# Layer 0 of a four-layer graph network: the order of the messages and the adjacency blocks on TensorE and ScalarE

## The chip, the core and the metric

One core of a Trainium2 chip runs the whole program in one launch. The metric is the device time of that launch in microseconds (us), as the median of repeated runs. The engines are PE (TensorE, matmuls), DVE (VectorE), ACT (ScalarE), POOL (GpSimd) and SP (SyncE, which here only starts transfers). Each has its own instruction queue and works it off in order; between engines there are only semaphores.

## The reference, cut to what matters

Four graph layers follow each other on 6250 nodes with 128 features and 106250 edges, sorted by target node. Each adds its result to x and normalizes the rows:

```python
edge_index = jnp.stack([src, dst])
x = _layernorm(x + _L0_gnn_ref(x, src, dst, edge_weight, L0_gnn_kernel, L0_gnn_bias), axis=-1)
x = _layernorm(x + _L1_gnn_ref(x, L1_gnn_bases, L1_gnn_relation_base_weights, src, dst, edge_type_64), axis=-1)
x = _layernorm(x + _L2_gnn_ref(x, edge_index, edge_type_2, ...), axis=-1)
x = _layernorm(x + _L3_gnn_ref(x, edge_index, L3_gnn_W1, L3_gnn_b1, L3_gnn_W2, L3_gnn_b2), axis=-1)
```

The change lies in layer 0, which sums over the *source* nodes what it reads at the targets:

```python
def _L0_gnn_ref(inp, edge_row, edge_col, edge_val, kernel, bias):
    support = jnp.matmul(inp, kernel)
    messages = edge_val[:, None] * support[edge_col]
    output = jax.ops.segment_sum(messages, edge_row, num_segments=N_NODES)
    return output + bias
```

The last layer is a graph convolution with two passes over the same edges, `segment_sum(h[src] * norm)`. The kernel computes both passes as dense products with an adjacency matrix, and that matrix is built during layer 0.

## The kernel before

**The loop of layer 0.** The edges lie in 832 tiles of 128. `Fori(0, NBODY)` runs over 52 bodies of 16 tiles; a body has four steps (`FSTEPS`), a step four tiles (`FT`) and two groups of two tiles (`FHALF`). All engines run this loop side by side, each with its own list.

What a step k of body i does for the messages:

- DVE makes `hits`, `sel` and `wS` (lines 1550 to 1560, `sel_ready`): which window column and which source row an edge has, with its weight. Then it finds duplicates of a source within a tile (1563, 1569) and writes the row numbers for the scatter (1573), which waits for `scatter_through`.
- PE, `window_by_edge` (1070): eight fp32 matmuls (four as written; the profile counts each fp32 matmul twice) give C, the weights of the window's nodes in each edge row, into bank 0 or 1. ACT, `keep_window` (723), copies C to SBUF.
- SP loads the window's rows of the support table (498). PE, `rows_to_add` (1080), multiplies C by them: the rows to add, bank 4 or 5, semaphore `messages`.
- ACT, `keep_rows` (728), copies them to SBUF. It waits for `scatter_through`: POOL must have come to the last scatter of step k-1, so that the scatters of step k-2, which used the same half of the buffer, have landed.
- POOL (629) issues four scatters with addition, one into each of four tables in HBM. Scatter t waits until the scatter of the same table of the step before has landed.

What it does for the adjacency, for each of its two groups n:

- DVE (1582, 1583, `ohot_ready`) makes one-hot masks in bf16, two tiles per group. There are two sets of mask buffers, so the masks of a group wait until the matmuls of the group two before are through (`ab_built`).
- PE, `build_adjacency` (1091), multiplies them in six matmuls into banks 3, 6 and 7. Each bank waits until ACT has copied the group before out of it (`ab_kept`).
- ACT, `keep_adjacency` (741), copies the three banks into a kept half in bf16, six copies per step.
- At the end of the body ACT starts the store of the half, 2352 KB (758). The two halves take turns; `adj_stored` guards their reuse.

Once a body DVE makes the type mask (1588) after the masks of step 0, PE multiplies it by the relation weights (`body_weights`, 1100) in step 1, and DVE reduces the result at the end of the body (1592). SP loads edge types (487, after the type mask of the body before) and source rows (491, after `sel_ready` of the body before), 512 KB each.

**Order around the change.** Each engine's order is written by hand. PE: `window_by_edge(0)`, and then for each step `build_adjacency(k)`, `window_by_edge(k + 1)`, in step 1 `body_weights`, `rows_to_add(k)`. ACT: `keep_window(0)`, and then for each step `keep_adjacency(k)`, `keep_window(k + 1)`, `keep_rows(k)`. DVE: selection and index write of step k, then its two groups of masks.

Of the kernel before, what the change touches and what calls it, by code (L numbers as in the profile page):

```python
# [49 lines left out]
FSTEPS = BODY // FT  # L50
# [57 lines left out]
def gnn_program(nc, src, src_row, dst, type2, type64, weight, x, xT0, k0, bias0, bases, rel_weights,  # L108
# [4 lines left out]
    with ctx:  # L113
# [3 lines left out]
        def sem(name):  # L117
            return ctx.enter_context(nc.semaphore(name))
# [214 lines left out]
        adj_stored = [sem(f"adj_stored{k}") for k in range(2)]  # L333
# [366 lines left out]
        def _(act):  # L700
# [19 lines left out]
            def keep_window(i, k):  # L720
                act.wait_ge(c_summed, i * FSTEPS + (k + 3))
                act.wait_ge(messages, i * FSTEPS + (k + 3))
                nc.scalar.activation(C[k % 2], bank[k % 2][0:W, :], ACT.Copy).then_inc(c_kept, 1)

            def keep_rows(i, k):
                act.wait_ge(messages, i * FSTEPS + (k + 5))
                act.wait_ge(scatter_through, i * FSTEPS + (k + 3))
                nc.scalar.activation(msg[k % 2].rearrange("p t f -> p (t f)"), bank[4 + k % 2][:, :],
                                     ACT.Copy).then_inc(msg_kept, 1)
# [6 lines left out]
            def keep_adjacency(i, u, k):  # L736
                for n in range(FHALF):
                    at = k * FHALF + n
                    for j, (bk, ha, hb) in enumerate(H_BANKS):
                        act.wait_ge(ab_built, i * (NHB * RING) + (NHB * (at + 2) + j + 1))  # L740
                        nc.scalar.activation(half_kept[u][:, ha:hb, at * W:(at + 1) * W],  # L741
                                             bank[bk][:, 0:(hb - ha) * W].rearrange("p (h w) -> p h w", w=W),
                                             ACT.Copy).then_inc(ab_kept, 1)
# [3 lines left out]
            with act.Fori(0, NCHUNK) as c:  # L747
                for u in range(2):
                    i = c * 2 + u
                    keep_window(i, 0)  # L750
                    act.wait_ge(adj_stored[u], c * 16 + 16)
                    for k in range(FSTEPS):
                        keep_adjacency(i, u, k)
                        if k < FSTEPS - 1:
                            keep_window(i, k + 1)
                        keep_rows(i, k)
                    act.wait_ge(ab_kept, i * (NHB * RING) + NHB * (RING + 1))
                    act.dma_start(adj[bass.ds(c * P, P), u * HB * HALF_COLS:(u + 1) * HB * HALF_COLS],
                                  half_kept[u].rearrange("p h c -> p (h c)")).then_inc(adj_stored[u], 16)
# [114 lines left out]
        def _(pe):  # L874
# [190 lines left out]
            def window_by_edge(i, k):  # L1065
                g = i * FSTEPS + k
                pe.wait_ge(sel_ready, g + (FSTEPS + 1))
                pe.wait_ge(c_kept, g + 1)
                for t in range(FT):
                    last = nc.tensor.matmul(bank[k % 2][0:W, t * P:(t + 1) * P], wS[:, k % 2, t, :], sel[k % 2][:, t, :],  # L1070
                                            start=True, stop=True)
                last.then_inc(c_summed, 1)

            def rows_to_add(i, k):
                g = i * FSTEPS + k
                pe.wait_ge(c_kept, g + 3)
                pe.wait_ge(xwin_in[k], i * (16 * FHALF) + 16 * FHALF)
                pe.wait_ge(msg_kept, g + 1)
                for t in range(FT):
                    last = nc.tensor.matmul(bank[4 + k % 2][:, t * P:(t + 1) * P], C[k % 2][:, t * P:(t + 1) * P],  # L1080
                                            xwin[k][t // GT], start=True, stop=True)
                last.then_inc(messages, 1)

            def build_adjacency(i, k):
                for n in range(FHALF):
                    at = k * FHALF + n
                    pe.wait_ge(ohot_ready, i * RING + (at + 1))
                    for j, (bk, ha, hb) in enumerate(H_BANKS):
                        pe.wait_ge(ab_kept, i * (NHB * RING) + (NHB * at + j + 1))
                        for t in range(GT):  # L1090
                            last = nc.tensor.matmul(bank[bk][:, 0:(hb - ha) * W], lo_hot[n * GT + t],  # L1091
                                                    hw_hot[n * GT + t][:, ha * W:hb * W], start=t == 0, stop=t == GT - 1)
                        last.then_inc(ab_built, 1)

            def body_weights(i):

                pe.wait_ge(hot_ready, i + 2)
                pe.wait_ge(alpha_ready, i + 1)
                for t in range(BODY):
                    last = nc.tensor.matmul(bank[2][:, t * NB * NPART:(t + 1) * NB * NPART], type_hot[:, t * P:(t + 1) * P],  # L1100
                                            relw_parts[:, :, :].rearrange("r b n -> r (b n)"), start=True, stop=True)
                last.then_inc(alpha_summed, 1)

            pe.wait_ge(relw_ready, 1)
            with pe.Fori(0, NBODY) as i:
                window_by_edge(i, 0)
                for k in range(FSTEPS):
                    build_adjacency(i, k)
                    if k < FSTEPS - 1:
                        window_by_edge(i, k + 1)  # L1110
                    if k == 1:
                        body_weights(i)
                    rows_to_add(i, k)
            pe.wait_ge(ab_kept, NHB * (NG + 1))
            flag = pe.value_load(flag_i[0:1, 0:1], min_val=0, max_val=1)
            with pe.If(flag != 0):
# [575 lines left out]
```

## Time and profile before

| | |
|---|---|
| median of 3 runs | 5966.51 us (5962.67 to 5968.96) |
| profiled execution | 5968.96 us, span 5967.3 us |
| mean granted clock of PE in the span | 0.717 |
| busy in the span: PE, DVE, ACT, POOL | 3830.2, 2201.3, 1009.9, 3073.7 us |
| loop of layer 0 | about 148 to 1922 us of the span |
| in it busy: PE, DVE, ACT, POOL | 1230.1, 1049.1, 745.7, 1309.9 us |
| in it DMA share, bytes moved | 0.63, 142 GB/s |

The span reaches from the first to the last instruction. Busy times are sums over instructions. The granted clock is a share of 2.4 GHz: 1.0 means 2.4 GHz, 0.5 means 1.2 GHz. A row of a timeline gives the start, the duration, engine and line, the operation, what it writes and reads, how many instructions are merged in it, and in brackets the idle time of the engine before it with what ended it. An engine name with a q (ACTq, SPq) is a queue that starts transfers. Lines are those of the kernel before.

### The profile page before, as it was taken

The numbers are of one execution on the slowest core, as the hardware profiler recorded it, in microseconds if no ns is written. First come the engines' busy times: TensorE is split into PE (matmuls) and PEld (weight loads), VectorE is DVE, ScalarE is ACT, GpSimd is POOL, SyncE is SP. The second block draws the span as 40 slices with busy tenths as digits, with TensorE's granted clock in tenths as the row PEclk, the third lists the DMA queues.
The fourth block names the chain that finished last, engine by engine and source line by source line (L and its number), as shares of the span: only waits on it lengthen the run. The fifth ranks groups of instructions, "written<-read, shape, count | busy, mean of one in ns | idle before, by whom it ended". The sixth has DMA issues, their size and how long they took to land. (4 is left out here: it accounts for less than half of the span.)

```text
span 5967.3 us, 90251 instructions
## 1 busy us (share of the span) xinstructions
PE 3830.2 (64%) x20675; PEld 2557.1 (43%) x20676; DVE 2201.3 (37%) x8525; ACT 1009.9 (17%) x2045; POOL 3073.7 (52%) x2549
## 2 busy tenths in 40 slices
PE   4677676676766244444454344444444999989998
PEld 3344333344333233433343333434334566656664
DVE  5566555565555433334343112222222111111122
ACT  2444443444443100000000000000000000000000
POOL 3777777777777666666666566666665000000000
PEclk7777767767676567677667555555555999989999
DMA  7666666666666511111111111111111666666664
GB/s 242 140 143 139 142 153 144 138 143 139 139 152 131 139 44 52 46 51 46 50 47 47 41 42 46 44 46 43 46 44 49 209 205 206 207 198 204 205 206 141
DMA packets 382424, 693.89 MB, mean 116 GB/s; under 512 B 56824, under 2 KB 233889, under 8 KB 371568
## 3 DMA queue, kind: packets, MB, share of 16 engines
q1 hardware_dynamic: 190180, 373.66, 20.9%
q0 software_dynamic: 176272, 185.39, 17.8%
q10 hardware_dynamic: 15804, 133.26, 5.5%
q14 instruction: 143, 1.17, 0.1%
q8 instruction: 25, 0.41, 0.0%
HBM read 474.67 MB, written 220.82 MB: 117 GB/s over the span
## 5 line engine op out<-in xcount | busy, mean ns | idle before, releaser
L589 POOL DMA_INDIRECT rows<-t,idx_ring x1664 | 1642.2, 987 | 953.5 <-issue 468.9
L629 POOL DMA_INDIRECT sums<-rows,idx_ring x832 | 1368.8, 1645 | 501.2 <-DMA sums<-rows,idx_ring 258.8
L927 PE MATMUL bank<-S,rows 128*128 128x192 f32 (+1 forms) x3328 | 914.6, 418 | 730.7 <-DVE arena L1264 485.6
L927 PEld LDWEIGHTS bank<-S,rows 128*128 128x128 f32 x3328 | 767.6, 291 | 862.2 <-DVE arena L1264 514.3
L1091 PE MATMUL bank<-arena 128*128 128x384 bf16 (+1 forms) x2496 | 675.0, 424 | 567.5 <-ACT acc L741 283.2
L1025 PE MATMUL bank<-alpha,arena 128*128 128x384 bf16 x5460 | 902.3, 327 | 0.0
L1025 PEld LDWEIGHTS bank<-alpha,arena 128*128 128x128 bf16 x5460 | 535.6, 98 | 353.9 <-issue 5.6
L1091 PEld LDWEIGHTS bank<-arena 128*128 128x128 bf16 x2496 | 242.1, 115 | 921.1 <-ACT acc L741 354.8
L924 PE MATMUL bank<-S,ones 128*1 128x24 f32 x1664 | 132.4, 210 | 714.8 <-DVE acc L1264 603.9
L1583 DVE TENSOR_SCALAR arena<-S 128x1176 bf16<-128x1176 int16 x832 | 455.8, 548 | 0.0
L1481 DVE TENSOR_TENSOR acc<-acc,bank 128x24 f32 x832 | 149.7, 180 | 802.8 <-issue 484.1
L1262 DVE TENSOR_TENSOR alpha<-alpha,bank 1x24 f32 x416 | 69.9, 168 | 916.9 <-remote 626.7
L924 PEld LDWEIGHTS bank<-S,ones 128*1 128x1 f32 x1664 | 68.0, 88 | 760.9 <-DVE acc L1264 639.3
L1582 DVE TENSOR_SCALAR arena<-S,arena 128x128 bf16<-128x128 int16 x832 | 238.9, 287 | 375.0 <-PE bank L1091 341.3
L1264 DVE TENSOR_TENSOR arena<-arena,bank 128x192 f32 x416 | 147.6, 355 | 605.4 <-issue 253.2
L666 POOL DMA_DIRECT2D arena<-xp_d x7 | 3.8, 559 | 703.6 <-DMA xp_d<-arena 703.6
L1070 PE MATMUL bank<-shared,wS 128*24 128x128 f32 x1664 | 321.8, 359 | 32.1 <-DVE wS L1558 32.1
L692 POOL DMA_DIRECT2D out<-xcur x12 | 9.1, 754 | 635.3 <-DVE xcur L1406 595.4
L1080 PE MATMUL bank<-rows,arena 24*128 24x128 f32 x1664 | 305.0, 335 | 0.0
L741 ACT ACTIVATE acc<-bank 128x384 bf16<-128x384 f32 (+1 forms) x624 | 277.2, 503 | 36.2 <-PE bank L1091 13.0
L741 ACT ACTIVATE xcur<-bank 128x384 bf16<-128x384 f32 (+1 forms) x624 | 275.4, 502 | 35.2 <-PE bank L1091 12.7
L1080 PEld LDWEIGHTS bank<-rows,arena 24*128 24x128 f32 x1664 | 258.1, 233 | 54.1 <-issue 52.6
(152 smaller groups left out, 3400.3 us busy)
## 6 DMA issues: line engine op xcount, KB each, us to landing
alpha<-adj SPq DMA_DIRECT2D x260, 672.0 KB, 4.3
adj<-xcur ACTq DMA_DIRECT2D x26, 2352.0 KB
adj<-acc ACTq DMA_DIRECT2D x26, 2352.0 KB
arena<-src_row SPq DMA_DIRECT2D x104, 512.0 KB
rows<-adj SPq DMA_DIRECT2D x52, 672.0 KB, 4.4
S<-adj SPq DMA_DIRECT2D x52, 672.0 KB, 4.3
arena<-type SPq DMA_DIRECT2D x52, 512.0 KB
rows<-t,idx_ring POOLq DMA_INDIRECT x1664
```

The lines of the kernel that those rows point to most:

```text
L589: nc.gpsimd.indirect_dma_start(out=rows[:, k, t, :], out_offset=None, in_=tables[p], in_offset=bass.IndirectOffsetOnAxis(ap=idx_ring[:, k, ...
L629: nc.gpsimd.indirect_dma_start(out=sums_t[t], out_offset=bass.IndirectOffsetOnAxis(ap=idx4[:, k, t:t + 1], axis=0), in_=msg[k % 2][:, t, : ...
L741: nc.scalar.activation(half_kept[u][:, ha:hb, at * W:(at + 1) * W], bank[bk][:, 0:(hb - ha) * W].rearrange("p (h w) -> p h w", w=W), ACT.C ...
L924: nc.tensor.matmul(count_at(k), ones[:, 0:1], of_group[:, t, 0:W], start=t == 0, stop=t == GT - 1)
L927: last = nc.tensor.matmul(bank[k % 2][:, 0:width], rows[:, k, t, :], of_group[:, t, 0:width], start=t == 0, stop=t == GT - 1)
L1025: last = nc.tensor.matmul(bank[c][:, 0:CHUNK_COLS].rearrange("p (s c) -> p s c", s=2), x_parts[:, q * PIECE_H + hh, part, :], adj_slot[q][ ...
L1070: last = nc.tensor.matmul(bank[k % 2][0:W, t * P:(t + 1) * P], wS[:, k % 2, t, :], sel[k % 2][:, t, :], start=True, stop=True)
L1080: last = nc.tensor.matmul(bank[4 + k % 2][:, t * P:(t + 1) * P], C[k % 2][:, t * P:(t + 1) * P], xwin[k][t // GT], start=True, stop=True)
L1091: last = nc.tensor.matmul(bank[bk][:, 0:(hb - ha) * W], lo_hot[n * GT + t], hw_hot[n * GT + t][:, ha * W:hb * W], start=t == 0, stop=t == ...
L1481: nc.vector.tensor_tensor(to, to, bank[c][:, n * W:(n + 1) * W], ALU.add).then_inc(added[p], 1)
L1582: nc.vector.tensor_scalar(lo_hot[n * GT + t], iota_hw[:, 0:P], lo_f[:, e], None, ALU.is_equal)
L1583: last = nc.vector.tensor_scalar(hw_hot[n * GT + t], iota_hw, hwi[:, e], None, ALU.is_equal)
```

## The change

On ACT, `keep_adjacency(i, u, k)` goes behind `keep_window(i, k + 1)` and `keep_rows(i, k)`, and the wait for the earlier store goes with it. On PE, `build_adjacency(i, k)` goes behind `window_by_edge(i, k + 1)`, `body_weights(i)` and `rows_to_add(i, k)`. DVE's, SP's and POOL's lists stay as they are, and so do all buffers and semaphores.

```diff
@@ -748,12 +748,13 @@
                 for u in range(2):
                     i = c * 2 + u
                     keep_window(i, 0)
-                    act.wait_ge(adj_stored[u], c * 16 + 16)
                     for k in range(FSTEPS):
-                        keep_adjacency(i, u, k)
                         if k < FSTEPS - 1:
                             keep_window(i, k + 1)
                         keep_rows(i, k)
+                        if k == 0:
+                            act.wait_ge(adj_stored[u], c * 16 + 16)
+                        keep_adjacency(i, u, k)
                     act.wait_ge(ab_kept, i * (NHB * RING) + NHB * (RING + 1))
                     act.dma_start(adj[bass.ds(c * P, P), u * HB * HALF_COLS:(u + 1) * HB * HALF_COLS],
                                   half_kept[u].rearrange("p h c -> p (h c)")).then_inc(adj_stored[u], 16)
@@ -1104,13 +1105,14 @@
             pe.wait_ge(relw_ready, 1)
             with pe.Fori(0, NBODY) as i:
                 window_by_edge(i, 0)
-                for k in range(FSTEPS):
-                    build_adjacency(i, k)
-                    if k < FSTEPS - 1:
-                        window_by_edge(i, k + 1)
+                for k in range(FSTEPS - 1):
+                    window_by_edge(i, k + 1)
                     if k == 1:
                         body_weights(i)
                     rows_to_add(i, k)
+                    build_adjacency(i, k)
+                rows_to_add(i, FSTEPS - 1)
+                build_adjacency(i, FSTEPS - 1)
             pe.wait_ge(ab_kept, NHB * (NG + 1))
             flag = pe.value_load(flag_i[0:1, 0:1], min_val=0, max_val=1)
             with pe.If(flag != 0):
```

## Rows read from the trace of the kernel before

**Rows 1.** Busy times by stretch: PE, PEld, DVE, ACT, POOL, granted clock, DMA share, GB/s.

```profile
148.00:1922.00 1774.00, 1230.10 (x6358) 697.69 (x6358) 1049.12 (x4245) 745.74 (x1591) 1309.90 (x796) 0.71 0.63 142
```

**Rows 2.** Groups by line, 148 to 1922 us: busy us, mean ns, idle before.

```profile
L629 POOL DMA_INDIRECT sums<-rows,idx_ring x796 | 1310.1, 1646 | 465.4 <-DMA sums<-rows,idx_ring 251.4 <-issue 201.5 <-DVE idx_ring L1573 9.1
...
L1588 DVE TENSOR_SCALAR arena<-arena,iota_p 64x2048 bf16<-64x2048 int32 x49 | 66.4, 1355 | 0.0
...
L1592 DVE TENSOR_REDUCE alpha<-bank 128x384 f32 x50 | 27.4, 547 | 0.0
```

**Rows 3.** Waits, 148 to 1922 us: who for whom, us in total, times, longest.

```profile
ACT rows L728 <- POOLq L628: 691.8, 161, 10.1
...
POOL sums L629 <- DMA sums<-rows,idx_ring: 251.4, 144, 5.7
...
POOL sums L629 <- ACT rows L728: 3.4, 11, 0.3
```

**Rows 4.** Timeline of ACT from 1006 us: keep_rows and copies behind it.

```profile
1006.50 0.60 ACT L728 ACTIVATE rows<-bank 128x512 f32<-128x512 f32 x1 [8.86 <-POOLq L628]
...
1009.73 0.49 ACT L741 ACTIVATE xcur<-bank 128x384 bf16<-128x384 f32 x1
```

**Rows 5.** Timeline of PE from 1007 us.

```profile
1007.55 2.14 PE L1091 MATMUL bank<-arena 128*128 128x408 bf16 x6 [8.36 <-ACT xcur L741]
...
1011.14 0.56 PE L1100 MATMUL bank<-relw_parts,arena 64*128 64x24 bf16 x16
...
1015.77 1.05 PE L1070 MATMUL bank<-shared,wS 128*24 128x128 f32 x8
1016.76 1.15 PE L1080 MATMUL bank<-rows,arena 24*128 24x128 f32 x8
1017.84 1.17 PE L1091 MATMUL bank<-arena 128*128 128x408 bf16 x6
...
1024.25 2.07 PE L1080 MATMUL bank<-rows,arena 24*128 24x128 f32 x8
1026.26 1.90 PE L1070 MATMUL bank<-shared,wS 128*24 128x128 f32 x8
```

**Rows 6.** Timeline of DVE from 1009 us.

```profile
1009.95 0.25 DVE L1582 TENSOR_SCALAR arena<-S,arena 128x128 bf16<-128x128 int16 x1 [1.73 <-PE bank L1091]
...
1011.25 0.24 DVE L1550 TENSOR_TENSOR hits<-iota_w,rel 128x96 f32<-128x96 f32 x1
...
1012.01 0.24 DVE L1558 TENSOR_TENSOR wS<-hits,wgt 128x96 f32<-128x96 f32 x1
...
1013.57 0.17 DVE L1573 TENSOR_TENSOR idx_ring<-dup,arena 128x4 int32<-128x4 f32 x1
```

**Rows 7.** Timeline of POOL around a store.

```profile
1029.71 1.55 POOL L629 DMA_INDIRECT sums<-rows,idx_ring  x1 [0.30 <-issue]
...
1043.83 1.74 POOL L629 DMA_INDIRECT sums<-rows,idx_ring  x1 [6.79 <-issue]
```

**Rows 8.** Timelines of SP's queue, ACT's queue and POOL, two bodies.

```profile
420.39 0.52 SPq L487 DMA_DIRECT2D arena<-type  x1
427.15 0.34 ACTq L758 DMA_DIRECT2D adj<-acc  x1
434.90 1.55 POOL L629 DMA_INDIRECT sums<-rows,idx_ring  x1 [1.40 <-DMA sums<-rows,idx_ring]
...
1028.79 0.53 SPq L487 DMA_DIRECT2D arena<-type  x1
1029.43 0.37 ACTq L758 DMA_DIRECT2D adj<-xcur  x1
```

**Rows 9.** Timeline of PE: builds after idle times of 2.2 to 2.9 us.

```profile
379.08 1.99 PE L1091 MATMUL bank<-arena 128*128 128x408 bf16 x6 [2.85 <-ACT xcur L741]
...
450.17 1.59 PE L1091 MATMUL bank<-arena 128*128 128x408 bf16 x6 [2.23 <-ACT xcur L741]
...
684.85 1.26 PE L1091 MATMUL bank<-arena 128*128 128x408 bf16 x6 [2.40 <-issue]
```

## The prediction

> **What bounds the kernel now.** The stages first: the change touches the loop over 52 bodies of layer 0, which fills 148 to 1922 us; nothing outside it changes. No engine is full there: PE is busy 1230 of 1774 us at a mean granted clock of 0.71, POOL 1310 [rows 1]. Then the groups of the stage: POOL issues 796 scatters of 1.646 us each in these 1774 us [rows 2]; at 16 a body, a body takes 16 x 1774 / 796 = 35.7 us. Between two undisturbed scatters POOL idles 0.30 us [rows 7], so its own work is 16 x 1.95 = 31.2 us a body. The missing 4.5 us stand in the waits: POOL waits 251.4 us for the landing of its own earlier scatters and only 3.4 us for ACT's rows, while ACT waits 691.8 us in keep_rows for POOL [rows 3]. One such landing per body is late. The store of 2352 KB starts at 1029.43, behind a load of types at 1028.79; the scatter of 1029.71 is caught with them, and its successor in the same table, four scatters on, starts only at 1043.83, after 6.79 us of idle time [rows 7, 8]. So today's path is POOL's 31.2 us plus one stall behind the store. Everything else runs ahead of POOL and waits for it; messages that are ready earlier are worth at most those 3.4 us.
>
> **What the change costs, part by part.** No instruction is added or removed. Three things move.
>
> ACT: keep_rows(k) comes ahead of keep_adjacency(k). It waits for POOL's release (POOL has entered the last scatter of step k-1). The six copies of keep_adjacency, formerly done before that wait, now lie behind it. By itself this costs nothing: ACT is busy 746 of 1774 us [rows 1]. What is queued behind the wait is what counts: the second group of build_adjacency(k) needs the copies of the first.
>
> PE and DVE: window_by_edge(k+1) and rows_to_add(k) come ahead of build_adjacency(k). On DVE, whose order is unchanged, the masks of step k+1's second group wait until build_adjacency(k)'s second group is through (two sets of mask buffers), and the selection for step k+2 stands behind those masks in the queue. Before, PE had build(k+1) to do while DVE made that selection. After, PE stands at window(k+2), first in its queue, until DVE has finished it. So a closed chain arises, which today's order does not have: build(k), second group -> masks(k+1) -> selection(k+2) -> window(k+2) -> rows_to_add(k+1) -> build(k+1), both groups.
>
> Its length from rows. Neighbours on PE overlap by some 0.07 us (1016.76 + 1.15 against 1017.84), which I take off each. At 1.2 GHz a window takes 1.83, rows_to_add 2.00, one group of build 2.07 us; at 2.4 GHz 0.98, 1.08 and 1.10 us [rows 5]. PE to DVE takes 0.26 us (1007.55 + 2.14 to 1009.95); masks of a group to the next operation 1.30 (1009.95 to 1011.25); selection until wS is written 1.00 (1011.25 to 1012.25); the way from DVE to PE, which no row shows alone, I take as the same 0.26, with 0.1 and 0.6 as bounds [rows 5, 6]. PE's gap per step is therefore 0.26 + 1.30 + 1.00 + 0.26 = 2.82 us. The second group can't start sooner than 1.05 us after keep_rows starts (1006.50 to 1007.55), which the first group covers [rows 4, 5].
>
> A step with 2.4 GHz throughout: 0.98 + 1.08 + 2 x 1.10 + 2.82 = 7.1 us. With 1.2 GHz throughout: 1.83 + 2.00 + 2 x 2.07 + 2.82 = 10.8 us. With the clock low after the gap and back for the second group: 9.8 us.
>
> Which of them holds depends on what such a gap does to the clock. Five gaps between 2.2 and 2.95 us began at full clock in the stage; after four of them the builds took 1.59 to 2.06 us, after one, of 2.40 us, they took 1.26 as at full clock; three of the five are in [rows 9]. I take the middle price, 9.8 us. *The Trainium skill ("TensorE: Matmul & The Clock Gate", HAM oscillation, the second failure mode) says that short idle times between groups of matmuls can make the clock swing between its two levels and that the kernel pays for each swing; the trace agrees with the four slow builds above. By that rule steps cost 9.8 us, without it 7.1.*
>
> A body has three intervals from one step's messages to the next that count. (1) From step 2 to step 0 of the next body DVE has two steps to do: builds 2.07 + 1.10, 0.26, masks 1.30, the reduction 0.55, selection to index write 2.49 (1011.25 to 1013.74), 0.26, two mask groups 2.60, the type mask 1.36, selection 1.00, 0.26, window and rows 3.83: 17.1 us [rows 2, 5, 6]. (2) To step 1: 9.8 and the weights' matmuls, 0.5: 10.3. (3) To step 2: 9.8. Sum 37.2 us. One gap in five without a fall takes 3 x 0.2 x 2.7 = 1.6 off; low spells that last on into the second group, at a guess one in three, put 3 x 0.33 x 0.97 = 1.0 on; each late message meets a slack of two scatters, some 3.5 us, only (that far ahead comes the release), so good and bad steps don't average fully, for which I put 0.4: 37.0 us.
>
> DMA stall: the store now goes out behind keep_rows(3) and six copies, some 3.9 us after the release instead of 0.2 (copies end at 1010.22 after the release at 1006.50, [rows 4]). That is two scatters later, so it catches the scatter that starts with it as before, and the caught one is due again at step 0, where messages are late anyway. The stall (4.5 us a body) is thus hidden under the chain rather than added to it. The loads wait for type mask and selection(1), which now come after the release: they go out 2 to 4 us behind the store.
>
> Sum: 37.0 - 35.7 = +1.3 us a body, 52 bodies, +68 us. The profiled execution took 5968.96 us (span 5967.3), the median is 5966.51: 6035 us, 1.1% slower.
>
> **Rivals.**
> A. The clock doesn't come back between gaps: 10.8 a step, body 18.1 + 11.3 + 10.8 = 40.2 us, +234 us: 6200. For it: rows_to_add and window were both slow from 1024.25 to 1028.16. Against it: after the slow build of 1007.55 rows_to_add at 1016.76 was fast [rows 5].
> B. No change: POOL and its stall stay the bound, body 35.7, 5966 us. With a step of x us the three intervals are (x + 7.3) + (x + 0.5) + x, which is 35.7 at x = 9.3; this holds if steps cost less than that. For it: POOL waits 3.4 us for ACT today; against it: PE gets three new gaps a body.
> C. Faster: the stall shrinks. Its price is set by what stands in the DMA queues with the store. In the one kind of body where the loads were issued 6.8 us ahead of the store (420.39 against 427.15), the caught scatter started 7.75 us after the store with 1.40 us idle time, against 14.4 and 6.79 us [rows 7, 8]. If the store, now 3.9 us later, is parted from the loads, some 1.5 us a body are saved: 34.2 us, -78 us: 5890. It decides only if the chain above is under 34.2 us a body, steps of 8.8 us by the same sum, so gaps must mostly leave the clock up. *The Trainium skill ("DMA: Bandwidth & Descriptors", Queues, rings and completion order) says that each DMA engine goes round its queues packet by packet, so less company in the queues means an earlier landing; the two landings above agree with it.*
>
> **How the numbers follow.** Forecast 0.55; A 0.12; B 0.13; C 0.20. Slower by over 0.2% (12 us, about what a measurement of this kernel can tell; the runs spread by 6 us) is 0.67, within it 0.13, faster 0.20. The forecast's own range is 5990 to 6110. With parts of A and C the range is 5900 to 6150: the ends leave out most of A and C's best bodies.
>
> **What the profile of the changed kernel would show.** Right: L1070's matmuls get idle time in front of them that DVE's wS ends, about 2.8 us for three of four steps (now none); ACT's wait in keep_rows for POOL falls from 692 us to under 300, and PE's L1080 ends it often; POOL's wait for ACT's rows rises from 3.4 us to 100 or more; the store follows keep_rows(3) by 3.7 us; stores 37 us apart; PEclk at 0.71 or lower. Wrong: PE not waiting at L1070 (then a dependence was misread); stores 35.7 us apart with POOL still waiting for DMA alone (B); caught scatters back within 10 us of the store (C). The likeliest error is the clock's answer to a 2.8 us gap, since each step hangs on it by 2.7 us; next the DVE to PE delay, 0.3 us a step or 50 us in all.

## The result and the profile after

The changed kernel takes 6063.83 us (median of 4, 6058.6 to 6067.31) against 5964.59 us of the kernel before (median of 4), a ratio of 1.0166 (95% interval 1.0148 to 1.0183): 99 us or 1.7% slower, where 68 us were forecast. Its profiled execution took 6085.72 us (span 6084.1), 22 us above that median, so the loop is read by itself.

First ACT's queue in the changed kernel, the second and the last of its 52 stores, one for each body:

```profile
145.02 0.35 ACTq L759 DMA_DIRECT2D adj<-acc  x1
...
2022.55 0.34 ACTq L759 DMA_DIRECT2D adj<-acc  x1
```

These are 50 bodies in 1877.5 us, 37.55 us each; before it was 35.7 [rows 1, 2]. 52 bodies with 1.87 us more each make 97 us, the whole difference of the medians. After the last store the two profiled executions differ by 16.7 us more (4061.5 against 4044.9 us), in passes whose code is the same; the other runs of the changed kernel don't show this.

The waits of the changed kernel between 148 and 2020 us (us in total, times, longest) answer to [rows 3]:

```profile
DVE arena L1584 <- PE bank L1092: 759.7, 235, 5.3
ACT arena L723 <- PE bank L1071: 696.9, 166, 6.3
PE bank L1071 <- DVE wS L1560: 513.5, 150, 5.2
...
ACT rows L728 <- PE bank L1081: 264.7, 198, 1.9
...
POOL sums L629 <- ACT rows L728: 243.4, 110, 3.5
POOL sums L629 <- issue: 210.7, 598, 3.4
POOL sums L629 <- DMA sums<-rows,idx_ring: 119.9, 84, 2.5
```

The picture of [rows 3] has turned round. ACT's 691.8 us of waiting in keep_rows for POOL are gone; it waits for PE's rows_to_add, and POOL waits 243 us for ACT, before 3.4. PE stands 513.5 us in front of the windows (L1071) until DVE has written wS, an entry that the kernel before doesn't have. DVE waits 760 us for the builds. That is a ring of engines that wait for each other, the closed chain.

One turn of it in PE's timeline, with the idle time ahead of a row in brackets:

```profile
1014.34 1.90 PE L1071 MATMUL bank<-shared,wS 128*24 128x128 f32 x8 [5.06 <-DVE wS L1560]
1016.16 2.07 PE L1081 MATMUL bank<-rows,arena 24*128 24x128 f32 x8
1018.17 3.71 PE L1092 MATMUL bank<-arena 128*128 128x408 bf16 x12
1024.62 1.81 PE L1071 MATMUL bank<-shared,wS 128*24 128x128 f32 x8 [2.75 <-DVE wS L1560]
1026.36 0.60 PE L1101 MATMUL bank<-relw_parts,arena 64*128 64x24 bf16 x16
1026.89 2.07 PE L1081 MATMUL bank<-rows,arena 24*128 24x128 f32 x8
1028.89 3.47 PE L1092 MATMUL bank<-arena 128*128 128x408 bf16 x12
1034.89 1.85 PE L1071 MATMUL bank<-shared,wS 128*24 128x128 f32 x8 [2.53 <-DVE wS L1560]
1036.67 2.07 PE L1081 MATMUL bank<-rows,arena 24*128 24x128 f32 x8
1038.68 3.69 PE L1092 MATMUL bank<-arena 128*128 128x408 bf16 x12
1042.30 1.15 PE L1081 MATMUL bank<-rows,arena 24*128 24x128 f32 x8
```

Three windows of the body have a gap in front of them. After each gap the window and rows_to_add run at 1.2 GHz (1.81 to 2.07 us, at full clock 1.05 and 1.15 [rows 5]). Within the twelve matmuls of the builds the clock comes back: they take 3.5 to 3.7 us, where two groups take 2.42 at full clock (those of step 3, at 1043.38) and one alone 2.14 at the low one [rows 5], and the rows at 1042.30 run at full speed. Of 151 windows in the loop with a gap over 1 us ahead of them, 150 took more than 1.4 us. In the kernel before, none of the windows between 148 and 1922 us has such a gap.

And the intervals, in ACT's timeline, from one keep_rows to the next:

```profile
1005.86 0.60 ACT L728 ACTIVATE rows<-bank 128x512 f32<-128x512 f32 x1 [0.54 <-PE bank L1081]
...
1008.96 0.35 ACTq L759 DMA_DIRECT2D adj<-xcur  x1
...
1018.27 0.60 ACT L728 ACTIVATE rows<-bank 128x512 f32<-128x512 f32 x1 [1.42 <-PE bank L1081]
...
1029.00 0.60 ACT L728 ACTIVATE rows<-bank 128x512 f32<-128x512 f32 x1 [1.94 <-PE bank L1081]
...
1038.78 0.60 ACT L728 ACTIVATE rows<-bank 128x512 f32<-128x512 f32 x1 [1.42 <-PE bank L1081]
...
1043.49 0.60 ACT L728 ACTIVATE rows<-bank 128x512 f32<-128x512 f32 x1 [0.54 <-PE bank L1081]
```

Step 2 to the next step 0 is 4.71 + 12.41 = 17.1 us, step 0 to 1 is 10.7, step 1 to 2 is 9.8; over the loop the means are 17.1, 10.4 and 10.0.

The stall behind the store has changed too. SP's queue and POOL after the store of 1008.96:

```profile
1013.44 0.53 SPq L487 DMA_DIRECT2D arena<-type  x1
1014.23 1.30 SPq L491 DMA_DIRECT2D arena<-src_row  x1
...
1017.74 1.54 POOL L629 DMA_INDIRECT sums<-rows,idx_ring  x1 [2.10 <-DMA sums<-rows,idx_ring]
```

The loads now go out 4.5 and 5.3 us behind the store, and the scatter that has to wait for the caught one starts 8.8 us after the store with 2.1 us of idle time. It is so in nearly every body (median 8.8 us, mean idle time 2.1 us). In the kernel before the median is 11.2 us and the mean idle time 4.4 us; the 14.4 us of [rows 7] are the longest of its 50 bodies.

The mean granted clock says nothing of all this: 0.71 in the loop before and 0.70 after, since before PE's idle time lay where nobody waited for it.

### The profile page after: what moved, and what is told of

The parts are those of the page before. It is cut to its first block and busy times, and to the rows that moved or that the text cites. A ratio compares the mean times of both kernels' runs of the same rounds, so it can differ in the third digit from the quotient of the medians.

```text
span 6084.1 us, 90251 instructions
## 1 busy us (share of the span) xinstructions
PE 3984.0 (65%) x20675; PEld 2685.2 (44%) x20676; DVE 2191.0 (36%) x8525; ACT 1041.9 (17%) x2045; POOL 3065.0 (50%) x2549
## 5 line engine op out<-in xcount | busy, mean ns | idle before, releaser
L629 POOL DMA_INDIRECT sums<-rows,idx_ring x832 | 1353.0, 1626 | 612.4 <-ACT rows L728 248.1
L928 PE MATMUL bank<-S,rows 128*128 128x192 f32 (+1 forms) x3328 | 928.1, 422 | 702.6 <-DVE arena L1266 348.4
L1071 PE MATMUL bank<-shared,wS 128*24 128x128 f32 x1664 | 335.0, 370 | 567.6 <-DVE wS L1560 564.2
L1092 PE MATMUL bank<-arena 128*128 128x384 bf16 (+1 forms) x2496 | 700.2, 449 | 0.0
L1071 PEld LDWEIGHTS bank<-shared,wS 128*24 128x24 f32 x1664 | 206.1, 134 | 685.8 <-issue 330.1
L1092 PEld LDWEIGHTS bank<-arena 128*128 128x128 bf16 x2496 | 285.9, 127 | 372.7 <-issue 270.7
L1081 PE MATMUL bank<-rows,arena 24*128 24x128 f32 x1664 | 382.7, 398 | 2.9 <-ACT arena L723 2.9
L1081 PEld LDWEIGHTS bank<-rows,arena 24*128 24x128 f32 x1664 | 326.9, 288 | 62.9 <-issue 61.3
```

The lines of the kernel that those rows point to most:

```text
L629: nc.gpsimd.indirect_dma_start(out=sums_t[t], out_offset=bass.IndirectOffsetOnAxis(ap=idx4[:, k, t:t + 1], axis=0), in_=msg[k % 2][:, t, : ...
L928: last = nc.tensor.matmul(bank[k % 2][:, 0:width], rows[:, k, t, :], of_group[:, t, 0:width], start=t == 0, stop=t == GT - 1)
```

## The experiments

Chips differ in the passes behind the loop (the kernel before took 5549 us on the chip of PE alone, of messages early with the window last, of the selection moved and of the first run of the store in three parts, and 5970 and 5980 us on the others'), so each ratio is against the kernel before on the same chip. Bodies are the mean distance of stores over the loop.

### Which engine's order: PE alone

PE has the changed order, ACT the old one.

```diff
-                for k in range(FSTEPS):
-                    build_adjacency(i, k)
-                    if k < FSTEPS - 1:
-                        window_by_edge(i, k + 1)
+                for k in range(FSTEPS - 1):
+                    window_by_edge(i, k + 1)
                     if k == 1:
                         body_weights(i)
                     rows_to_add(i, k)
+                    build_adjacency(i, k)
+                rows_to_add(i, FSTEPS - 1)
+                build_adjacency(i, FSTEPS - 1)
```

> Only TensorE's order is changed; ScalarE keeps its old one (copies of the adjacency, window, rows). Theory of the closed chain (second build group, masks, selection, window, rows_to_add, build): the chain runs over PE and DVE alone, so it is there in full, with gaps of 2.5 to 5 us in front of three windows a body, and the stores stand 37 to 37.7 us apart: ratio to before 1.013 to 1.018. Rival, that the loss comes from ScalarE, whose copies now stand behind its wait for POOL: without that part the stores stand 35.7 us apart, ratio 1.000.

Measured: 1.0191 (1.0174 to 1.0208), body 37.58 us; the ratio lies just above the range expected, the body in it. PE waits for DVE's wS as in the full change (410.5 us, 150 times). ACT's new order, with the copies behind the wait for POOL, is not the cause: PE's half alone gives the whole loss. ACT's half alone was not run.

In this kernel only 95 of the 150 windows with a gap over 1 us ahead of them were slow. The clock still fell in every step, in the other 55 only within the window or behind it, and it came back later: from the start of the window to the end of the builds a step without the weights takes 7.47 us in the median, in the changed kernel too. So it is this stretch, and not the window alone, that shows the price of the clock.

### Messages early, window last

```diff
                 for k in range(FSTEPS):
-                    build_adjacency(i, k)
-                    if k < FSTEPS - 1:
-                        window_by_edge(i, k + 1)
                     if k == 1:
                         body_weights(i)
                     rows_to_add(i, k)
+                    build_adjacency(i, k)
+                    if k < FSTEPS - 1:
+                        window_by_edge(i, k + 1)
```

ACT likewise: keep_rows, copies, keep_window.

> Both engines do rows_to_add(k), then the adjacency of step k, then window(k+1). Messages are as early as in the change and the copies stand behind the wait for POOL as there, but window(k+2) now comes behind build(k+1), so DVE has a build's time for the selection. Chain theory: no idle time ended by DVE's wS in front of the windows, body 35 to 36 us, ratio 0.995 to 1.003. Rival, that the copies behind the wait for POOL (or the store 4 us later) cost the time: still 37 us or more, ratio 1.013 or more.

Measured: 1.0025 (1.0014 to 1.0037), body 36.05 us. No idle time in front of a window is ended by wS any more. The order keeps two things of the change, early messages and a store after the copies, and neither costs 1.7%: what is left is 0.25%.

### The changed kernel with the selection ahead of the second mask group

Against the changed kernel, DVE's list alone differs: `selection`, `row_numbers` and `masks` hold the same instructions as before.

```diff
+                selection(0)
                 for k in range(FSTEPS):
-                    selection(k)
                     row_numbers(k)
                     masks(k, 0)
+                    if k < FSTEPS - 1:
+                        selection(k + 1)
                     masks(k, 1)
```

> The changed kernel with one move on DVE: the selection of step k+1 stands ahead of the second mask group of step k, within a body. It takes the link masks to selection out of the chain. Chain theory: the gaps of 2.5 to 2.8 us in front of windows 2 and 3 vanish, that in front of window 1 (5 us, with the type mask) as well, and POOL is the bound again: body 35 to 36 us, ratio to before 0.995 to 1.003. Rival (loss on ScalarE or from the later store): nothing changes, ratio 1.015.

Measured: 0.9919 (0.9903 to 0.9936), body 34.85 us. The chain theory's direction holds, and the size goes beyond what it expected: this is faster than the kernel before. Its waits between 500 and 1500 us:

```profile
ACT rows L728 <- POOLq L628: 339.0, 67, 9.3
...
POOL sums L629 <- DMA sums<-rows,idx_ring: 101.6, 69, 5.7
...
PE bank L1071 <- DVE wS L1560: 36.1, 36, 1.6
```

ACT waits for POOL again, so POOL is the bound. PE has 45 gaps over 1 us in front of windows, 1.3 us in the mean, where the changed kernel has 151 with 3.4 us, and only one of the 45 windows took more than 1.4 us. With the chain gone something of the change is a gain. POOL's wait for landings hints where: 101.6 us in this stretch, 139.0 us in the same stretch of the kernel before. Later experiments look at the stall.

### The gap filled with matmuls that nobody needs

The changed kernel, with 12 matmuls in front of window 1 and 6 in front of windows 2 and 3 (24 and 12 in the profile, which counts each twice). No dependence is changed, work is only added.

```diff
+            def fill(n):
+                for _ in range(n):
+                    nc.tensor.matmul(bank[2][:, 384:512], ones[:, :], ident[:, :], start=True, stop=True)
...
                 window_by_edge(i, 0)
+                fill(12)
                 for k in range(FSTEPS - 1):
...
                     build_adjacency(i, k)
+                    if k < FSTEPS - 2:
+                        fill(6)
```

> The changed kernel with matmuls of two constant tiles (fp32, 128 columns, results unused) put where TensorE would idle: 12 in front of window 1, 6 in front of windows 2 and 3. The chain of dependences is untouched, only the idle time is filled. Theory that a step costs 9.8 us because the clock falls in the gap: the clock stays at 2.4 GHz, a step costs 7.1 us, POOL is the bound again, stores 35 to 36 us apart, ratio to before 0.99 to 1.003, though PE does more work. Rival, that the gap of 2.8 us alone makes the chain the bound: at full clock too 36.5 us or more, ratio 1.01 or more.

Measured: 0.9873 (0.9833 to 0.9913), body 34.23 us, faster than was expected. PE's timeline in this kernel (L1107 is the filler):

```profile
1034.30 1.50 PE L1107 MATMUL bank<-ident,ones 128*128 128x128 f32 x12
1036.99 1.05 PE L1071 MATMUL bank<-shared,wS 128*24 128x128 f32 x8 [1.19 <-DVE wS L1567]
1037.98 0.56 PE L1101 MATMUL bank<-relw_parts,arena 64*128 64x24 bf16 x16
1038.46 1.15 PE L1081 MATMUL bank<-rows,arena 24*128 24x128 f32 x8
1039.55 2.42 PE L1092 MATMUL bank<-arena 128*128 128x408 bf16 x12
```

PE still waits for wS, but only 1.19 us after the filler, and all that follows in this step runs at 2.4 GHz: from the start of the window to the end of the builds, with the weights, it takes 4.98 us, where the changed kernel needs 7.74 from 1024.62. It is not so in every step: of 85 windows with a gap over 1 us, 9 took more than 1.4 us, and in 34 more steps the clock fell behind the window; 42 ran at full clock to the end of the builds. The granted clock in 500 to 1500 us is 0.89. Against the same order without the filler (1.0166 and 1.0149, each beside its own runs of the kernel before) useless work takes 2.7 to 2.9% off the time: without the fall of the clock the gap does not make the chain the bound. The rival, that the gap alone is enough, falls.

### The store in three parts, on the kernel before

The store of 2352 KB is cut along the blocks and issued behind keep_rows of steps 0, 1 and 2 of the next body. So it is both cut and moved; the experiment after this one only moves it.

```diff
+            PARTS = ((0, 17), (17, 33), (33, 49))
...
                     keep_rows(i, k)
+                    if k < len(PARTS) and not first:
+                        if k == 0:
+                            act.wait_ge(ab_kept, i * (NHB * RING) + NHB)
+                        store_part(c if u else c - 1, 1 - u, k)
-                    act.wait_ge(ab_kept, i * (NHB * RING) + NHB * (RING + 1))
-                    act.dma_start(adj[bass.ds(c * P, P), u * HB * HALF_COLS:(u + 1) * HB * HALF_COLS],
-                                  half_kept[u].rearrange("p h c -> p (h c)")).then_inc(adj_stored[u], 16)
```

> The kernel before with the store of 2352 KB cut in three along the blocks (about 800 KB each), issued behind keep_rows of steps 0, 1 and 2 of the next body. If POOL's path before was 31.2 us of its own work and one stall of 4.5 us behind the store, each part now lands before the next scatter of the same table is due (7.4 us later), the stall goes, and the body falls to 31.5 to 33 us: ratio 0.965 to 0.978. If the stall comes from the sum of bytes and not from the size of one store, it stays in parts: 35 us or more, ratio 0.995 to 1.0.

Measured: 0.962 (0.9604 to 0.9636), 212 us less and a little more than was expected, and again 0.963 (0.961 to 0.965) on another chip. Busy times and waits of this kernel (the stretch 148 to 1700 us, then the waits of 500 to 1500 us):

```profile
148.00:1700.00 1552.00, 1186.97 (x6302) 682.26 (x6301) 1040.15 (x4225) 745.90 (x1569) 1307.66 (x786) 0.75 0.74 161
```

```profile
ACT rows L728 <- POOLq L628: 373.2, 113, 5.5
...
POOL sums L629 <- issue: 123.9, 401, 0.8
...
POOL sums L629 <- DMA sums<-rows,idx_ring: 21.1, 66, 0.8
```

786 scatters in 1552 us are 31.6 us a body; POOL waits 21 us for landings in 1000 us. This bears out the prediction's reading of the kernel before, 31.2 us of POOL's work and one stall of 4.5 us behind the store: the bytes are the same, the stall is gone.

### The whole store later, on the kernel before

The helper is that of the experiment before, with one part of all 49 blocks; the store at the end of the body is gone here too.

```diff
                     if k < FSTEPS - 1:
                         keep_window(i, k + 1)
+                    if k == 0 and not first:
+                        act.wait_ge(ab_kept, i * (NHB * RING) + NHB)
+                        store_part(c if u else c - 1, 1 - u, 0)
                     keep_rows(i, k)
```

> The kernel before with the whole store moved behind the copies of step 0 and the window 1 of the next body, ahead of keep_rows(0), some 4 to 5 us later; all else as before. Theory that the stall depends only on the size of the store (the caught scatter moves along with it): ratio 0.997 to 1.003. Rival C of the prediction, that a store parted from the loads of types and source rows gives a shorter stall (the caught scatter back 8 us after the store instead of 13): body 33.5 to 34.5 us, ratio 0.975 to 0.99.

Measured: 0.9847 (0.9807 to 0.9887), body 34.01 us. Timeline of SP's and ACT's queues and of POOL in this kernel:

```profile
478.16 0.53 SPq L487 DMA_DIRECT2D arena<-type  x1
478.88 0.43 SPq L491 DMA_DIRECT2D arena<-src_row  x1
482.94 0.34 ACTq L755 DMA_DIRECT2D adj<-acc  x1
491.94 1.54 POOL L629 DMA_INDIRECT sums<-rows,idx_ring  x1 [2.46 <-DMA sums<-rows,idx_ring]
```

The loads now go out 4.8 us ahead of the store, and the scatter that waits for the caught one starts 9.0 us after it. Over the loop the median is 9.1 us, against 11.2 in the kernel before, and the mean idle time 2.4 us against 4.4; the 14.4 us of [rows 7, 8] are the extreme. The kernel before shows the same within itself: in the four bodies whose loads went out 5.7 to 6.8 us ahead of the store it was 7.8 to 8.7 us, in the others with loads, at most 1.9 us ahead, 7.9 to 14.4 with one only under 9. So rival C had the right mechanism in the kernel before: a store parted from the loads gives a shorter stall. Of the 3.8% that the store in three parts brings, 1.5% come with the move of the whole store alone.

### The changed kernel with the store in three parts

> The changed kernel with the store cut in three, as in the kernel that took 0.962 with it. If in the changed kernel the stall behind the store is hidden under the chain, the cut brings nothing here: stores' bodies still 37 to 37.6 us, ratio to before 1.013 to 1.018. If the stall still added to the body, the ratio falls to about 0.98.

Measured: 1.0115 (1.0074 to 1.0156), body 37.1 us. Its waits between 500 and 1500 us:

```profile
PE bank L1090 <- DVE wS L1579: 260.9, 80, 5.2
...
POOL sums L629 <- ACT rows L728: 176.1, 76, 3.5
...
POOL sums L629 <- DMA sums<-rows,idx_ring: 6.7, 22, 0.3
```

The stall is gone (6.7 us in 1000, before the cut 59.9), and POOL waits for ACT instead. The chain is the bound; the same cut that brings 3.8% without it brings about 0.5% here, less than the intervals can tell. To size that, it ran once more beside the changed kernel on one chip:

> The changed kernel once more, on one chip with the three that follow, since chips differed in the later passes. Ratio 1.015 to 1.019.

> The changed kernel with the cut store. Its profile showed bodies of 37.1 us against 37.55 and POOL waiting 13 us for landings instead of 120. So some 0.4 us a body of the stall's 4.5 were not hidden: ratio 0.003 to 0.005 under that of the changed kernel. If the stall was hidden entirely, the two ratios agree within 0.001.

Measured: 1.0149 (1.0127 to 1.017) and 1.0124 (1.0102 to 1.0147). The difference has the expected sign and is a little under the 0.003 expected, but the intervals overlap; 18.7 us between the medians are 0.36 us a body. The first two profiles have bodies of 37.55 us without and 37.1 with the cut. Those of this chip have 37.6 and 36.9, but here the profiled executions are the slowest and the fastest of their four, so they overstate it.

### Both together: is the early message worth anything?

The changed order with the selection moved ahead, and the cut store.

> The changed kernel with the selection ahead of the second mask group, and with the store cut in three. Without the chain and without the stall POOL's own 31.2 us are the only bound: body 31.4 to 32 us, ratio 0.960 to 0.964, the same as the kernel before with the cut store. If messages that are ready earlier are worth something of their own, it is below that by more than 0.3%.

It gave 0.9628 (0.9587 to 0.9668), and with the kernel before and the cut store on the same chip:

> The kernel before with the cut store, again: 0.960 to 0.965.

> The changed order with the selection moved ahead and the cut store. If POOL's own work is the only bound of both, the ratio is that of the run before this one within 0.002. If earlier messages are worth something of their own, it is lower by 0.003 or more.

Measured: 0.963 (0.961 to 0.965) and 0.9649 (0.9627 to 0.9671), 5756.35 and 5769.6 us. Without chain and stall both orders stand on POOL's own work (bodies of 31.5 and 31.8 us), and the early message brings nothing. That the moved selection alone was faster than the kernel before thus came from its shorter stall. The version that beats both kernels of this case is the old order with the store in three parts.

## Why the prediction was right, and where it was off

**What bounds the kernel before.** Right: POOL's work and one stall behind the store. The cut store removed 4.1 us of the 4.5 us a body.

**The closed chain.** Right in its place and in its terms. The intervals, summed from rows, were 17.1, 10.3 and 9.8 us; measured are 17.1, 10.7 and 9.8 in the body shown, and 17.1, 10.4 and 10.0 in the mean. That it runs over PE and DVE and not over ACT's wait is shown by PE's order alone (1.0191) and by the kernel with the selection moved (0.9919).

**The clock after a gap.** The choice of 9.8 us a step was right, and the filled gap shows that it decides the sign: at full clock the same chain no longer bounds. *The rule of the Trainium skill that the prediction weighed ("TensorE: Matmul & The Clock Gate", HAM oscillation, the second failure mode), a swing between two clock levels when TensorE is often idle for a short time between groups of matmuls, agrees with the 150 of 151 slow windows.*

Mis-sized was the step that followed. From five gaps, four with a fall, I took one gap in five without a fall, -1.6 us a body; in the changed kernel no step behind such a gap ran at full clock. The five came from the kernel before, whose bodies differ from one to the next, where those of the changed kernel are much alike; whether that is why was not tested.

The plain sum was 37.2 us, with the three corrections 37.0, and 37.55 was measured. Term by term, in means over the loop: the two groups of builds took 3.66 us together and were priced at 3.2, since the clock came back later than between the groups. With 0.07 us taken off for the overlap, that is 1.3 us a body over three steps, and it is what the allowance of 1.0 us for low spells that last stood for: right in kind, a little small. Against it, the gaps of steps 2 and 3 were 2.6 us and not 2.82, and the interval across the body's end came out at 17.1 although its builds took longer, so its other parts were priced some 0.5 us too high; together that is 0.9 us. The 0.4 us for poor averaging has no counterpart in the trace. Against the forecast that makes 1.6 + 0.3 - 0.9 - 0.4 = 0.6 us. So the forecast came close partly by luck: most of the 1.6 us was made up by parts priced too long and by an allowance that wasn't needed. 0.55 us in 52 bodies is 29 us, the distance between forecast (+68) and measurement (+99), within rounding.

**The stall hidden under the chain.** Right in the outcome: the cut store brings some 0.4 us a body where it brings 4.1 without the chain. But the stall that was hidden wasn't the 4.5 us that the prediction carried over. The store followed keep_rows(3) by 3.1 us (3.7 forecast) and the loads followed the store by 4.5 us (2 to 4 forecast), and with the two so far apart the stall held POOL for 2.1 us in the mean, 0.3 of which are there between any two scatters.

**The rivals.** A (clock never back) didn't happen: in each body it came back within the builds. B (no change) fell with the chain. C (a shorter stall) came true in its mechanism and not in its time. Its sign, a caught scatter back within 10 us of the store, stands in the changed kernel's trace (8.8 us), but its own condition, a chain under 34.2 us, wasn't met, so it could not show in the time. Where the chain is out of the way or absent it does: bodies of 34.23 us with the filled gap, 34.85 with the selection moved, 34.01 with the later store in the old order, against C's 34.2. Its price of 1.5 us a body was stated without its working, so this closeness is not evidence for a sum.

**Open.** The kernel with messages early and window last has its store as late as the one with the selection moved, and its loads also 2 to 3 us behind it in most bodies, yet its body is 36.05 us and not 34.85; POOL waits 134 us for landings in 1000 us, against 102. What keeps its stall longer was not taken apart. The way from DVE to PE was taken as 0.26 us; gaps of 2.5 to 2.75 us against the sum of 2.82 speak for no more than that, but it was not measured by itself.

## What to carry to other kernels

Before two groups are swapped in an engine's queue, look for what the *other* engines do meanwhile: here the build that was moved was what PE did while DVE prepared the next window, and without it the two formed a ring though neither was full. Sum that ring from rows at both clock levels. If the two sums lie on either side of the present bound, the clock in the pauses decides, and some throw-away matmuls in them are a cheap test. When a queue waits for the landing of its own small transfers, look at what large transfer went out just ahead of them. Here it was cut in parts that landed before the next wait was due, which was worth 3.8%, more than any order of the matmuls.

## What the runs showed of the hardware that was not expected

- Six or twelve unneeded fp32 matmuls per gap (12 or 24 in the profile) raised the granted clock between 500 and 1500 us from 0.70 to 0.89 and took 2.7 to 2.9% off the changed kernel's time.
- The mean granted clock stayed at 0.71 and 0.70 while the kernel became 1.7% slower: what counts is whether the slow matmuls lie on the path.
- After gaps of 2.5 us and more the fall of the clock came at different places, ahead of the window or within and behind it (150 of 151 windows slow in the changed kernel, 95 of 150 with PE's order alone), yet the stretch from window to builds took 7.47 us in the median in both (a step without the weights), against 4.49 us at full clock in the filled kernel.
- Behind a store of 2352 KB, the scatter that waits for a caught one started 7 to 14 us after the store, by what else is queued: 11.2 us in the median with 1 MB of loads mostly within 2 us ahead of it, 9.1 us with the store moved behind the loads, 8.8 us with the loads 4.5 us behind. With the same bytes in three parts POOL never waited over 0.8 us for a landing (500 to 1500 us).
